# Attention projection: the transposed input's remainder on GpSimd, the last rotated pair finished inside the first maxima, and value tiles of 17 columns

## The reference

```python
xn = layernorm(x)                       # no weights
qkv = xn @ qkv_w.T + qkv_b              # 256 -> 768
q, k, v = heads of qkv                  # 4 x 16 x 1024 x 16
q, k = rotary(q), rotary(k)             # x * cos + rotated(x) * sin
attn = softmax(q @ k.T * 16 ** -0.5)
x = x + (attn @ v) @ proj_w.T + proj_b
```

## Time and profile before

| | before |
|---|---|
| time, median of 3 runs | 1239.58 us (1237.76 to 1241.81) |
| the profiled execution, its time | 1242.32 us |
| its span, first to last instruction | 1240.50 us |
| mean granted TensorE clock | 0.925 |
| PE busy | 1092.3 us (88%) |
| DVE busy | 1041.1 us (84%) |
| ACT busy | 767.3 us (62%) |
| POOL busy | 345.9 us (28%) |
| projection | 0 to 125 us |
| first maxima | 125 to 157 us |
| attention | 157 to 820 us |
| cross-attention, routing, experts | from 820 us |

### The profile page before, as it was taken

How to read it: one execution, slowest core, us unless ns; L and a number is a source line. 1 busy time by engine, 2 the same in 40 slices (tenths; PEclk the granted TensorE clock), 3 DMA queues, 4 the chain that set the end, 5 groups by cost and what they waited for, 6 DMA issues and landing times. The chain is left out here.

```text
span 1240.5 us, 24360 instructions
## 1 busy us (share of the span) xinstructions
PE 1092.3 (88%) x8474; PEld 607.4 (49%) x8474; DVE 1041.1 (84%) x2147; ACT 767.3 (62%) x930; POOL 345.9 (28%) x313
## 2 busy tenths in 40 slices
PE   4776899999999998999999999988875039999996
PEld 4665433333333332333333333347764028888996
DVE  8998999999999997999999999636975986666652
ACT  3443078888788886788887888854553104655653
POOL 1544932112211220221022000022200021875673
PEclk9889589999999999999999999989985559999999
DMA  6879466234413440441344000035522021555442
GB/s 214 270 229 346 105 132 120 63 71 84 83 30 70 84 84 18 80 83 42 58 85 82 20 12 19 14 103 197 186 86 85 5 68 46 133 157 126 106 110 30
DMA packets 85654, 121.96 MB, mean 98 GB/s; under 512 B 24032, under 2 KB 57568, under 8 KB 84512
## 3 DMA queue, kind: packets, MB, share of 16 engines
q1 hardware_dynamic: 66288, 70.07, 18.7%
q0 software_dynamic: 15984, 39.86, 16.9%
q10 hardware_dynamic: 3264, 10.49, 2.3%
HBM read 77.24 MB, written 42.21 MB: 96 GB/s over the span
## 5 line engine op out<-in xcount | busy, mean ns | idle before, releaser
L754 DVE TENSOR_REDUCE b_max_halves<-banks 128x1 f32<-128x512 f32 x1024 | 632.2, 681 | 20.6 <-PE banks L821 20.4
L696 ACT ACTIVATE b_probs<-banks 128x1024 f32<-128x1024 f32 x512 | 520.4, 1026 | 166.8 <-PE banks L873 166.5
L821 PE MATMUL banks<-b_k,b_q 62*128 62x512 f32 x1024 | 402.0, 473 | 16.4 <-DVE b_max L771 10.1
L873 PE MATMUL banks<-b_q,b_k 64*128 64x512 f32 x1024 | 386.8, 459 | 5.0 <-issue 4.1
L843 PE MATMUL banks<-b_probs,b_v 128*32 128x256 f32 (+1 forms) x3840 | 322.3, 408 | 0.2 <-ACT b_probs L696 0.2
L873 PEld LDWEIGHTS banks<-b_q,b_k 64*128 64x128 f32 x1024 | 156.5, 186 | 219.9 <-issue 168.5
L821 PEld LDWEIGHTS banks<-b_k,b_q 62*128 62x128 f32 x1024 | 162.0, 191 | 51.2 <-DVE b_max_halves L754 39.4
L843 PEld LDWEIGHTS banks<-b_probs,b_v 128*32 128x32 f32 x3840 | 76.1, 108 | 167.8 <-issue 100.1
L498 POOL TENSOR_TENSOR b_att<-b_out,b_rec_spread 128x512 f32<-128x512 f32 x32 | 41.1, 1284 | 310.7 <-DMA b_rec_spread<-reciprocals 310.5
L430 POOL DMA_DIRECT2D b_q<-q_stacks x60 | 31.8, 532 | 247.5 <-PE banks L843 226.2
L1757 DVE TENSOR_TENSOR e_hTl<-e_hT,e_hTh 128x512 fp32r<-128x512 f32 x64 | 47.7, 745 | 48.9 <-ACT e_hT L1503 48.9
(11 more groups left out here) (244 smaller groups left out, 1481.4 us busy)
## 6 DMA issues: line engine op xcount, KB each, us to landing
e_w<-in_w SPq DMA_DIRECT2D x16, 1024.0 KB, 7.3
v_tiles<-a_v ACTq DMA_DIRECT2D x8, 1024.0 KB, 6.2
q_stacks<-a_parts SPq DMA_DIRECT2D x32, 256.0 KB, 5.0
k_stacks<-a_parts SPq DMA_DIRECT2D x32, 256.0 KB, 4.0
b_q<-q_stacks POOLq DMA_DIRECT2D x30, 256.0 KB, 6.2
b_k<-k_stacks POOLq DMA_DIRECT2D x30, 256.0 KB, 6.9
b_v<-v_tiles POOLq DMA_DIRECT2D x15, 512.0 KB, 9.3
b_q<-b_max_rows SPq DMA_DIRECT2D x256, 2.0 KB
```

The costliest lines, as they stand in the source:

```text
L696: nc.scalar.activation(pr[:, S % NP, u], ps[:, 2 * u:2 * u + 2, :], ACT.Exp, scale=D ** -0.5).then_inc(s_ex[u], 1)
L754: v.tensor_reduce(mxp[:, (k // NB) % 2, s, p, t, kh:kh + 1], ps[:, bank(last), :], AX.X, ALU.max)\
L821: nc.tensor.matmul(ps[:, bank(last), :], qs[g][stack, p, at:at + P], ks[g][stack, p, CH * kh:CH * kh + CH], start=True, stop=True).then_in ...
L873: return nc.tensor.matmul(ps[:, 2 * u + s, :], ks[g][stack, u, P * kt:P * kt + P], qs[g][stack, u, CH * h:CH * h + CH], start=True, stop=True)
```

## The change

The remainder of the transposed input is computed by GpSimd. It cannot read PSUM, so ScalarE also copies the transposed input unrounded to a new tile `xf` (128x1024), after the copies that round it, and when GpSimd has finished with the chunk before; GpSimd does one subtraction of 128x1024 from it. On GpSimd the remainder of chunk c + 1 stands between the additions of pairs 2c and 2c + 1. VectorE's order in a chunk becomes: rotate(2c), split(2c - 1), roots, moments, rotate(2c + 1), split(2c), moments.

The last two pairs (14 and 15) are finished in the attention's prologue. Pair 14's sum and pair 15's two products are written straight into `parts` (they wait there for the stores of chunk 5); in the attention, GpSimd adds pair 15 and subtracts the leading part of both (`end_sums`), ScalarE copies pair 15's leading part (`end_leading`), SP stores pairs 13, 14 and 15 (`end_stores`). The bias of v is multiplied and added inside the last chunk.

A head's place in the value tiles is VS = 17 columns: 16 of v and one of ones. The whole tile is filled with ones at the start, in place of zeros and a column of ones. The results of a head are still 32 partitions apart; the 15 between, which no product writes any more, are cleared once by VectorE ahead of the first maxima (`ps[:, PV, :]`, one bank), and TensorE's first maxima no longer wait for `b_max` to be cleared.

```diff
+VS = 17
@@ project_qkv @@
+        xf = sb("a_xnT", [P, KC, CH])
+        def whole(n, m):
+            s = n % 2
+            return parts[:, 2 * s:2 * s + 2, m, half(n // 2)]
+        def end_sums(g, pool):
+            n, k = 2 * J - 2, 2 * J - 1
+            g.tensor_tensor(whole(k, 1).bitcast(F32), whole(k, 0).bitcast(F32), whole(k, 1).bitcast(F32), ALU.add).then_inc(s_end, 1)
+            pool.wait_ge(s_end, 1)
+            g.tensor_tensor(whole(n, 1), whole(n, 1).bitcast(F32), whole(n, 0).bitcast(F32), ALU.subtract).then_inc(s_end, 1)
+            pool.wait_ge(s_end, 3)
+            g.tensor_tensor(whole(k, 1), whole(k, 1).bitcast(F32), whole(k, 0).bitcast(F32), ALU.subtract).then_inc(s_end, 1)
+            pool.wait_ge(s_end, 4)
+        def end_leading(act):
+            k = 2 * J - 1
+            act.wait_ge(s_end, 1)
+            nc.scalar.activation(whole(k, 0), whole(k, 1).bitcast(F32), ACT.Copy).then_inc(s_end, 1)
-        def last_stores(sp):
+        def end_stores(sp):
+            store_pair(sp, 2 * J - 3)
+            sp.wait_ge(s_end, 4)
+            store_pair(sp, 2 * J - 2)
             store_pair(sp, 2 * J - 1)
@@ ScalarE, take @@
                 for k in range(KC):
-                    last = nc.scalar.activation(xh[:, c % 2, k, :], ps[:, k, :], ACT.Copy)
+                    nc.scalar.activation(xh[:, c % 2, k, :], ps[:, k, :], ACT.Copy)
+                after(act, s_xe, c)
+                for k in range(KC):
+                    last = nc.scalar.activation(xf[:, k, :], ps[:, k, :], ACT.Copy)
                 last.then_inc(s_xh, 1)
@@ VectorE @@
-            def trailing(c):
-                dve.wait_ge(s_xh, c + 1)
-                for k in range(KC):
-                    last = v.tensor_tensor(xl[:, c % 2, k, :], ps[:, k, :], xh[:, c % 2, k, :].bitcast(F32), ALU.subtract)
-                last.then_inc(s_xe, 1)
+                if n == 2 * J - 1:
+                    dve.wait_ge(s_qs[(J - 1) % 2], 128 * ((J - 1) // 2))
+                    by = whole(n, 0).bitcast(F32), whole(n, 1).bitcast(F32)
-            v.memset(vsb[:], 0.0).then_inc(s_v0, 1)
-            dve.wait_ge(s_v0, 1)
-            v.memset(vsb[:, :, :, :, D:D + 1], 1.0).then_inc(s_v0, 1)
+            v.memset(vsb[:], 1.0).then_inc(s_v0, 1)
-            trailing(0)
                 rotate(2 * c)
+                if c:
+                    split(2 * c - 1)
                 if c % 2 == 0 and c + 2 < J:
                     spread(c + 2, 2)
-                if c:
-                    split(2 * c - 1)
-                if c + 1 < J:
-                    trailing(c + 1)
...
+                if c == J - 1:
+                    dve.wait_ge(s_bvb, 3)
+                    v.tensor_tensor(cw["bp"][:], ps[:, 0, 0:C], cw["bp"][:], ALU.add)
                 rotate(2 * c + 1)
-                split(2 * c)
+                if c < J - 1:
+                    split(2 * c)
...
-            dve.wait_ge(s_vp, 2 * J + 1)
-            v.tensor_tensor(cw["bp"][:], ps[:, 0, 0:C], cw["bp"][:], ALU.add)
-            split(2 * J - 1)
@@ GpSimd @@
+            def trailing(c):
+                pool.wait_ge(s_xh, c + 1)
+                g.tensor_tensor(xl[:, c % 2], xf[:], xh[:, c % 2].bitcast(F32), ALU.subtract).then_inc(s_xe, 1)
+                pool.wait_ge(s_xe, c + 1)
+            pool.wait_ge(s_clear0, 2)
+            trailing(0)
-            for n in range(2 * J):
+            for n in range(2 * J - 1):
...
+                if n == 2 * J - 2:
+                    pool.wait_ge(s_qs[(J - 1) % 2], 128 * ((J - 1) // 2))
+                    to = whole(n, 1).bitcast(F32)
...
+                g.tensor_tensor(to, by_even[:, q], by_odd[:, q], ALU.add).then_inc(s_eo, 1)
+                if q == 0 and n // 2 + 1 < J:
+                    pool.wait_ge(s_eo, n + 1)
+                    trailing(n // 2 + 1)
@@ load_group @@
-                     vst[b][:, :, G * VW * g:G * VW * g + G * VW]).then_inc(s_ld, 16)
+                     vst[b][:, :, G * VS * g:G * VS * g + G * VS]).then_inc(s_ld, 16)
@@ attend @@
             ones(0)
+            end_stores(sp)
             sp.wait_ge(s_ra, 1)
             rows(0, 0)
...
-                    if first and hg == 0:
-                        last_stores(sp)
...
+            end_leading(act)
             bodies(act, body)
...
             pool.wait_ge(s_minus, 1)
+            end_sums(g_, pool)
...
+            v.memset(ps[:, PV, :], 0.0)
             v.memset(mx[:], 0.0).then_inc(s_zero, 1)
...
-                    last = nc.tensor.matmul(ps[VW * j:VW * j + VW, PV, at], vs[hg // 2][:, kt, j, :],
+                    last = nc.tensor.matmul(ps[VW * j:VW * j + VS, PV, at], vs[hg // 2][:, kt, j, :],
...
-            pe.wait_ge(s_zero, 1)
```

More of the change, by code:

```diff
@@ L130, in project_qkv @@
         s_ev = sem("a_even_product")
[L131 removed]
+        s_vp = sem("a_v_product")
         s_vc = sem("a_v_copied")
@@ L185, in _ @@
             sp.dma_start(bv[:], wts["bvqkv"]).then_inc(s_wp, 16)
-            for c in range(J):
+            for c in range(J - 1):
                 sp.wait_ge(s_pb, 2 * c + 1)
                 store_pair(sp, 2 * c)
-                if c == J - 1:
+                if c == J - 2:
                     continue
@@ L232, in split @@
                     after(act, s_qs[c % 2], 128 * (c // 2))
-                nc.scalar.activation(parts[:, 2 * s:2 * s + 2, 0, half(c)], eo[:, n % 2], ACT.Copy).then_inc(s_pa, 1)
+                summed = whole(n, 1).bitcast(F32) if c == J - 1 else eo[:, n % 2]
+                nc.scalar.activation(whole(n, 0), summed, ACT.Copy).then_inc(s_pa, 1)
             def refill(c):
@@ L304, in split @@
                 dve.wait_ge(s_pa, n + 1)
[L305 to L310 removed]
+                v.tensor_tensor(whole(n, 1), eo[:, n % 2], whole(n, 0).bitcast(F32), ALU.subtract).then_inc(s_pb, 1)
+            v.memset(vsb[:], 1.0).then_inc(s_v0, 1)
             moments(0)
@@ L398, in _ @@
                 pair(2 * c)
+                if c == J - 1:
+                    pe.wait_ge(s_bvb, 2)
+                    pe.wait_ge(s_wp, 64)
+                    for k in range(KC):
+                        last = mm(ps[:, 0, 0:C], bvb[:, k, :], cw["wp"][:, k, :], start=(k == 0), stop=(k == KC - 1))
+                    last.then_inc(s_bvb, 1)
                 values(2 * c)
@@ L403, in _ @@
                 values(2 * c + 1)
-            pe.wait_ge(s_bvb, 3)
-            pe.wait_ge(s_wp, 64)
-            for k in range(KC):
-                last = mm(ps[:, 0, 0:C], bvb[:, k, :], cw["wp"][:, k, :], start=(k == 0), stop=(k == KC - 1))
-            last.then_inc(s_vp, 1)
-    return last_stores
+    return end_sums, end_leading, end_stores
 LD = 9 * 16
@@ L524, in rows, with attend @@
         sp.dma_start(self.xs[:, j % 2], x[j // 2, j % 2].rearrange("t p c -> p t c")).then_inc(self.s_xi[j % 2], 16)
-def attend(nc, ps, ident, group0, s_clear0, stores, last_stores, tail, firsts, cw, s_cw, x, ost, wts, qst, kst, vst):
+def attend(nc, ps, ident, group0, s_clear0, stores, ends, tail, firsts, cw, s_cw, x, ost, wts, qst, kst, vst):
     ctx = ExitStack()
@@ L538, in attend @@
         ks = [group0[1]] + [sb(f"b_k{g}", [P, 2, L], F32R) for g in range(1, NG)]
-        vs = [group0[2]] + [sb(f"b_v{g}", [P, KT, G, VW]) for g in range(1, NG)]
+        vs = [group0[2]] + [sb(f"b_v{g}", [P, KT, G, VS]) for g in range(1, NG)]
         NP = 4
@@ L617, in pair @@
             return s, kh, t, p
+        end_sums, end_leading, end_stores = ends
         block = ctx.enter_context(nc.Block())
```

30 lines of the change are left out of this document (15 added, 15 removed).

## The result

The kernel after takes 1228.26 us (median of 10 runs, 1225.35 to 1237.03) against 1237.70 us for the kernel before on the same chip (10 runs). The ratio is 0.993, with a 95% interval of 0.9907 to 0.9954. Two later sets of runs of the same two kernels, on two other chips, gave 1230.55 against 1238.81 (0.9927, 0.9901 to 0.9953) and 1231.82 against 1240.51 (0.9928, 0.9900 to 0.9957). The change brings 8.3 to 9.4 us; forecast were 8.5, and 1231.1 us for the time.

What follows compares the result with a forecast made beforehand. VectorE, hardly idle and excluding GpSimd, was taken to fill the projection; TensorE to pace the attention. From the median of 1239.58 us, 4.5 for the earlier start (remainder's cost included) and 4.0 for the columns gave 1231.1, range 1226 to 1240.

Steps and rivals of the forecast that it cites:

- The remainder: Projection: moving the remainder from VectorE to GpSimd was to cost 1.8 us, bounds -4 and +7.
- The walk: Projection: chunks stepped through with assumed durations, GpSimd's addition 2.35 us; eighth rotation at about 111.0 instead of 109.24.
- the two waits that were named: Projection, chunks with roots: roots wait about 2 us for GpSimd's addition, then another 2.3 for the remainder; 1.1 us lost.
- The late chunks: Projection: each takes 10.2 us instead of 10.7, winning about 0.4; over 11.5 us would make the prediction wrong.
- The last pairs: Projection's end: last pair finished in the first maxima, attention starts at 120.6 instead of 125.11; 4.5 us gained, remainder's cost included.
- Nothing for the covered work: First maxima: added GpSimd, ScalarE and SP work costs nothing; first load issued 15.5 us after the start, scores at 30.5.
- Rival D: Attention's start: first group's load lands late, scores wait 5 to 9 us, about 1238 us in all; chance 8%.
- 17 columns: Attention: exposed weight loads 12 ns shorter, 5.6 us, counted as 4.0, bounds 0 and 17; smaller v transfers counted as nothing.
- A: Attention: weight loads were hidden, groups keep 20.50 us, only the tail pays, 1235.1 us; chance 25%.
- B: First maxima: granted clock stays near 1.00 until the scores, some 2.5 us more gained, 1228.6 us; chance 10%.
- C: Projection: GpSimd's third operation holds splits or roots up in seven chunks, 16.5 us lost, 1247.6 us; chance 12%.
- E: Projection: remainder reaches TensorE when it did, ScalarE's copies replacing VectorE's wait; a share of C, no chance of its own.

Runs made afterwards that it cites:

- after31: The kernel after with value tiles and weights of 31 columns instead of 17: 1234.43 us against 1238.81 for the kernel before (0.9964).
- lastpairs32: The kernel after with 32 columns and the remainder back on VectorE, only the last pairs moved: 1232.40 us against 1240.44 for the kernel before (0.9936).
- again2: The kernel after, unchanged, run a third time: 1231.82 us against 1240.51 for the kernel before.
- lastpairs17: The kernel after with the remainder and root steps back as before; 17 columns and moved last pairs stay: 1225.48 us against 1240.51 (0.9886).
- remainder31: The kernel before with the remainder on GpSimd and tiles of 31 columns: 1241.01 us against 1240.44 (1.0007).
- weights17: The kernel before with 17 of 32 columns as weights of the values products, tiles and transfers unchanged: 1234.70 us against 1238.81 (0.9969).
- roots: The kernel after with roots moved ahead of the first rotation or behind their chunk's second: 1225.50 us against 1240.44 for the kernel before (0.9887).
- both17: The kernel lastpairs17 with the edit of roots: 1220.24 us against 1240.51 for the kernel before (0.9835).
- tiles17: The kernel before with 17 columns throughout (v's tiles, stores, loads and weights): 1228.35 us against 1238.81 (0.9923).
- weights24: The kernel before with 24 of 32 columns as weights of the values products: 1234.94 us in a single run.

## Why the prediction was right, and where it was not

**The total** was right: 8.5 us forecast, 8.3 to 9.4 measured. That it fits so well is luck: the start was forecast too early and the columns too low, and the two errors cancel.

**What bounds the kernel** stood: in the attention TensorE sets the pace, since narrower weights shortened the group; VectorE and GpSimd exclude each other in the projection. VectorE's 19.9 us a group are not reached at 20.28.

**The remainder** was mis-sized, at 1.8 us. The walk had the eighth rotation at 111.0, a loss of 1.8 us. Measured in this profile are 112.40, a loss of 3.2; against the five kernels of the experiments that have the remainder on VectorE and the roots in their place (107.43, 107.53, 107.59, 107.89, 108.16) it is 4.7, within the bounds of -4 and +7. The cost by the start is 3.5 (*after31* against *lastpairs32*), 4.2 (*again2* against *lastpairs17*), 6.0 with the last pairs in their old place (*remainder31* against *weights17*) and 2.3 with the roots moved (*roots* against *both17*). By its own steps:

- The chunk with roots between the fifth rotation (76.21, forecast 76.7) and the sixth chunk's (90.00) took 13.8 us; forecast were 12.8 + 1.1 = 13.9. Right, by the two waits that were named.
- The late chunks were to take 10.2 us. They took 10.7 (90.00 to 100.72) and 11.7 (to 112.40), the second of them over the 11.5 that the prediction named as a sign of being wrong. Here the walk failed. It let GpSimd's additions take 2.35 us, but an addition that follows a split waits for it in turn: 3.15, 3.13 and 3.27 us in these chunks. And it let ScalarE copy the transposed input as soon as it was there. In the sixth chunk ScalarE's copy for the pair before stands first and waits for the long addition (89.18 to 92.33). The transposes end at 91.5, but are copied from 93.80 on, and GpSimd, idle for 0.99 us, gets the unrounded copy only at 96.00. In the seventh it is GpSimd's own queue: the copies end at 107.4, and the remainder waits for the addition of 104.47 until 107.82, 0.4 us. The forecast priced the exclusion on VectorE's side only, although the row for the additions already had 2.82 us on average. ScalarE's and GpSimd's timelines, kernel after:

```profile
92.36 1.06 ACT L261 ACTIVATE a_parts<-a_rotated 128x1024 fp32r<-128x1024 f32 x1 [3.70 <-POOL a_rotated L388]
93.80 1.08 ACT L240 ACTIVATE a_xnT_leading<-banks 128x512 fp32r<-128x512 f32 x2
94.76 1.10 ACT L243 ACTIVATE a_xnT<-banks 128x512 f32<-128x512 f32 x2
```

```profile
96.00 2.36 POOL L371 TENSOR_TENSOR a_xnT_trailing<-a_xnT,a_xnT_leading 128x1024 fp32r<-128x1024 f32 x1 [0.99 <-ACT a_xnT L243]
```

- That lateness then went along with a lower clock. TensorE's timeline, kernel after, seventh chunk:

```profile
98.41 0.50 PE L415 MATMUL banks<-a_xnT_leading,a_w_leading 128*128 128x512 f32 x1 [2.73 <-POOL a_xnT_trailing L371]
98.75 0.39 PE L415 MATMUL banks<-a_xnT_leading,a_w_trailing 128*128 128x512 f32 x1
...
100.41 0.63 PE L415 MATMUL banks<-a_xnT_leading,a_w_leading 128*128 128x512 f32 x1
100.84 0.63 PE L415 MATMUL banks<-a_xnT_leading,a_w_trailing 128*128 128x512 f32 x1
```

TensorE had waited 2.73 us for the remainder; a few products later they follow each other in 0.43 us instead of 0.23, which is the lower of the two clock levels, for seven products, some 1.4 us. That is most of what the 11.7 us have over 10.2. The same dip stands in both other profiles of this kernel (clock 0.80 and 0.53 from 98 to 104 us). In *roots*, *lastpairs17* and *both17* that window is at 1.00; the dip one chunk before, from 86 to 92 us, is in *lastpairs17* as well as here (0.74 and 0.75). In the kernel after, each of TensorE's five waits of 2.1 to 3.0 us for the remainder is followed by such products, and neither of those of 0.46 and 0.74 us. In *roots* a wait of 1.94 us (before 93.53) is followed by none. So that the wait caused this dip is read from the order of the rows, not shown.

**The last pairs.** The forecast's 4.5 us were net of the remainder's 1.8, so 6.3 for this part. With the remainder on VectorE it is worth less (*lastpairs32* starts 5.0 earlier than *weights17*, *lastpairs17* 4.8 earlier than *tiles17*), with it on GpSimd more (*after31* starts 7.5 earlier than *remainder31*). Net of the remainder the two profiles show 3.85 of the 4.5 (start 121.26, forecast 120.6), and against *weights17*, whose projection is the old one, only 1.5.

**Nothing for the covered work** was right: load issued 15.5 us after the start, scores at 30.1. Rival D is out.

**17 columns** were undersized. The products' columns: 5.6 us worked out, 4.0 counted for fear of VectorE's pace, 4.1 measured by *weights17* alone and 5.65 in the attention's rows of the first profile. The rule of the Trainium skill by which the term would be 0 (TensorE: Matmul & The Clock Gate, "Step-by-step: what each phase is for") gave the wrong time: loads of 108, 101 and 95 ns come with 20.50, 20.40 and 20.36 us. Whether its conditions are met here, and whether the load or the product gave the time back, no run shows. The transfers, counted at nothing: *tiles17* is 6.4 us faster than *weights17* by the medians, of which the traces place 0.9 at the start and 3.8 in the attention, with the doubt told there. The Trainium skill's minimum of 512 B per transfer for full rate (DMA: Bandwidth & Descriptors, "Specifications") decided nothing here: *tiles17* is slower in no stage, and moves 114.09 MB where *weights17* moves 121.96. It was hardly tried either. *tiles17* has only 1024 more packets under 512 B (25056 against 24032), as many as one load of v has pieces of 272 B, and there are sixteen such loads.

**The parts do not add up,** and that stays largely open. By the medians the columns bring 10.5 us to the kernel before (*tiles17*), 3.9 to *after31* (1234.43 to 1230.55 on one chip) and, against the kernel before on their own chips, take *lastpairs32*'s 8.0 to *lastpairs17*'s 15.0. The 0.9 us at the start is missing between *after31* and the kernel after (121.29 and 121.26), but 0.7 is there between *lastpairs32* and *lastpairs17* (117.79 and 117.06). One interval between rows of maxima, the sixteenth, took 28.24 us in *after31* and 29.8 to 30.7 in the twelve other profiles, so some 2 us of its short attention are one execution's. The rest I can't place, and the cross stage's swing is as large as what is left.

**The base.** The profiled execution of before was long in the projection too: start 125.11, where *weights17* and *weights24*, which have the same projection, start at 122.79 and 122.94. So the difference of the two profiles (3.85 us) flatters this part, by some 2.2 us, as the cross stage belittles the rest. The forecast for the start was worked out on that longer projection, too. The medians are less exposed to both, but not free of them: of the kernel after's 31 runs, from 1224.08 to 1237.26 us, eleven took over 1233.

**The rivals.** A fell by *weights17*. B did not happen: the clock of the first maxima was 0.53, 0.57 and 0.55 in the three profiles of the kernel after. C named the right mechanism, the third operation on GpSimd, at 16.5 us; up to the start it costs 2.3 to 6.0. E is a part of it: the remainder reaches TensorE later than before, not sooner.

## What to carry to other kernels

Where two engines exclude each other, moving work from one to the other takes nothing off what they share: with the remainder alone moved, 10.3 us of work left VectorE, its busy time fell by 0.6 us (107.53 to 106.96), and the eighth rotation came 4.9 us later. Look at both engines' means against their undisturbed durations, and move small chains of operations to a stretch where the other engine is idle before moving a large one across. When a change bundles several parts, time each alone: here one part alone came out as fast as the whole, and the kernel without one of the others was faster by 6.3 us in the median (4.2 by its start).

## What was not expected of the hardware

- A step of 8 elements on VectorE was held for 2.2 to 2.4 us more than once in one chain, each time that GpSimd had another operation running: six times in this projection. The other way about, GpSimd's 2.35 us become 3.1 to 3.3 behind a split of 1.2.
- A weight load takes longer per column even where the loads are short: 0.87 ns for each of the 15 columns saved (108 to 95 ns). The attention's period followed, by 0.14 us of the 0.20 that 15 blocks with one exposed load each would give (*weights17*).
- Two profiles of one kernel differ by 9.7 us in a single stage (134.01 and 143.71) at equal instructions, by the granted clock (0.86 and 0.79). A difference of that size between two single profiles is no evidence of a change.
